# Attention block with two layer norms: the transpose of an iteration's row maxima placed behind the first turn of the next iteration

## What is computed

```python
x = x + attention(layernorm(x), Wq, Wk, Wv, Wo, bo)    # 16 heads of 16, causal softmax, scale 0.25
x = x + ffn(layernorm(x), rhs)

def ffn(lhs, rhs):        # rows of lhs and columns of rhs rounded to int8 by their largest magnitude
    acc = q_lhs @ q_rhs
    return acc * lhs_scale * rhs_scale
```

## Time and profile before

| | us |
|---|---|
| median of 3 runs | 1652.0 |
| lowest and highest | 1650.38, 1652.75 |
| the profiled execution, its own time | 1652.5 |
| its span, first to last instruction | 1650.7 |
| PE busy | 1562.4 (95%) |
| DVE busy | 1523.9 (92%) |
| ACT busy | 1363.3 (83%) |
| POOL busy | 275.4 (17%) |
| reductions of the max pass (line 356): 960 into `pmax`, 128 into `pblk` | 1101.0 and 151.8 |

### The profile page before, as it was taken

How to read it: one execution, slowest core, us unless ns; L and a number is a source line. 1 busy time by engine, 2 the same in 40 slices (tenths; PEclk the granted TensorE clock), 3 DMA queues, 4 the chain that set the end, 5 groups by cost and what they waited for, 6 DMA issues and landing times.

```text
span 1650.7 us, 40675 instructions
## 1 busy us (share of the span) xinstructions
PE 1562.4 (95%) x16715; PEld 623.3 (38%) x16715; DVE 1523.9 (92%) x1839; ACT 1363.3 (83%) x2659; POOL 275.4 (17%) x394
## 2 busy tenths in 40 slices
PE   5999999999999999999999999999999999999965
PEld 3555433333333333333333333333333333444433
DVE  5889989999999999999999999999999999488876
ACT  3656579999999999999999999999999999777641
POOL 3334201211112020202020202020202020100120
PEclk9999989999999999999999999999999999999986
DMA  3464301111211121212121212121212241035431
GB/s 112 149 195 141 107 23 35 35 35 34 61 47 61 47 69 47 64 45 67 47 61 48 73 37 77 34 77 36 77 29 79 46 139 34 32 107 160 146 106 62
DMA packets 105684, 118.84 MB, mean 72 GB/s; under 512 B 20696, under 2 KB 87580, under 8 KB 105500
## 3 DMA queue, kind: packets, MB, share of 16 engines
q1 hardware_dynamic: 105500, 116.25, 24.1%
HBM read 66.81 MB, written 48.76 MB: 70 GB/s over the span
## 4 chain that ended last, share of the span: by engine, by line
DVE 56%; PE 28%; ACT 1%; issue 1%; DMA 0%; SPq 0%; POOL 0%; DVEq 0%; ACTq 0%
DVE pmax L356 47%; PE psum L1155 12%; PE psum L1136 6%; DVE pblk L356 4%; PE psum L1196 3%; PE psum L264 3%; PE psum L278 2%; PE psum L283 2%; DVE V L1459 1%; DVE V L1440 1%; DVE V L1447 1%; DVE f_amax L1465 1%; ACT prob L1328 1%; PE psum L1220 1%; PE psum L1209 0%
## 5 line engine op out<-in xcount | busy, mean ns | idle before, releaser
L1328 ACT ACTIVATE prob<-psum 128x512 f32<-128x512 f32 (+1 forms) x2304 | 1180.8, 575 | 139.5 <-PE psum L1136 116.0
L356 DVE TENSOR_REDUCE pmax<-psum 128x2 f32<-128x1024 f32 (+1 forms) x960 | 1101.0, 1216 | 13.7 <-PE psum L283 7.0
L1155 PE MATMUL psum<-prob,V 128*32 128x256 f32 x8704 | 677.3, 391 | 0.0
L1136 PE MATMUL psum<-Q,K 50*128 50x512 f16 (+3 forms) x2560 | 465.9, 350 | 3.7 <-PEq L480 1.1
L1394 POOL TENSOR_SCALAR_AFFINE_SELECT prob<-prob 128x512 f32<-128x512 f32 x256 | 159.7, 636 | 1186.8 <-ACT prob L1328 1184.2
L264 PE MATMUL psum<-K,Q 48*128 48x512 f16 x1536 | 298.6, 385 | 12.6 <-DVE pmax L356 12.6
L1155 PEld LDWEIGHTS psum<-prob,V 128*32 128x32 f32 x8704 | 181.6, 108 | 294.9 <-issue 214.6
L1136 PEld LDWEIGHTS psum<-Q,K 50*128 50x128 f16 x2560 | 174.6, 94 | 251.5 <-ACT prob L1328 184.2
L264 PEld LDWEIGHTS psum<-K,Q 48*128 48x128 f16 x1536 | 74.3, 93 | 257.9 <-DVE pmax L356 209.7
L356 DVE TENSOR_REDUCE pblk<-psum 128x8 f32<-128x1024 f32 x128 | 151.8, 1219 | 5.9 <-PE psum L283 5.8
L283 PE MATMUL psum<-K,Q 48*128 48x512 f16 (+3 forms) x1024 | 128.5, 298 | 0.0
(11 more groups left out here) (122 smaller groups left out, 697.2 us busy)
## 6 DMA issues: line engine op xcount, KB each, us to landing
f_x<-in_L_attn_x SPq DMA_DIRECT2D x32, 512.0 KB, 5.2
unnormalised<-ust SPq DMA_DIRECT2D x64, 256.0 KB, 2.8
q_parts<-part SPq DMA_DIRECT2D x64, 128.0 KB
k_parts<-part SPq DMA_DIRECT2D x64, 128.0 KB
Q<-q_parts SPq DMA_DIRECT2D x128, 64.0 KB, 2.5
K<-k_parts SPq DMA_DIRECT2D x128, 64.0 KB, 2.1
out<-V SPq DMA_DIRECT2D x16, 512.0 KB, 3.3
f_rs<-inverse_sums SPq DMA_DIRECT2D x28, 256.0 KB
```

Source lines behind the costliest of these rows:

```text
L356: nc.vector.tensor_reduce(to, of, axis=AX.X, op=ALU.max).then_inc(M.mx_free, 1)
L1136: m = nc.tensor.matmul(PS[:, SB + i % RING, at:at + n], K[it % 2][rows, pair, kb * P:(kb + 1) * P], Q[it % 2][rows, pair, (c + 1) * CH - n ...
L1155: m = nc.tensor.matmul(PS[32 * h:32 * h + 32, UB, to:to + n], V[:, it // NG * NT + kb, col:col + 32], prob[(it * NSTEP + k) % PRING][:, h, ...
L1328: nc.scalar.activation(prob[g % PRING][:, h, 0:n], PS[:, SB + i % RING, 0:n], ACT.Exp, scale=by).then_inc(exp_done, 1)
```

## The change

The order of `TURNS` changes. The tail of iterations 1 to 14 moves from behind its own last turn to behind the first turn of the next iteration. The tails of iterations 0 and 15 stay. `TURNS` keeps its length, `BEFORE` its rows. DVE still combines the maxima directly behind the last turn of an iteration: at the first turn of the next one, ahead of its reduction (`combined_before` says at which turn which combination stands).

```diff
     for it in range(ITS):
-        turns += [(it, kind) for kind in (KINDS if it else sorted(KINDS, key=lambda kind: max(chunks_of(kind))))]
-        tail.append(len(turns))
-        turns.append((it, None))
+        for i, kind in enumerate(KINDS if it else sorted(KINDS, key=lambda kind: max(chunks_of(kind)))):
+            turns.append((it, kind))
+            if it >= 2 and i == 0:
+                tail.append(len(turns))
+                turns.append((it - 1, None))
+        if it in (0, ITS - 1):
+            tail.append(len(turns))
+            turns.append((it, None))
     return turns, tail
+
+
+def combined_before(n):
+
+    if TURNS[n][1] is None:
+        return TURNS[n][0] if TURNS[n][0] in (0, ITS - 1) else None
+    return TURNS[n + 1][0] if TURNS[n + 1][1] is None and TURNS[n + 1][0] < TURNS[n][0] else None
...
-assert sum(row[0] + row[2] for row in BEFORE) == TAIL[1] - TAIL[0] and sum(row[1] for row in BEFORE) == len(BLOCKS)
+assert sum(row[0] + row[2] for row in BEFORE) == TAIL[2] - TAIL[1] and sum(row[1] for row in BEFORE) == len(BLOCKS)
...
-    base = TAIL[0] + 1 + AHEAD + it * (TAIL[1] - TAIL[0])
+    base = TAIL[0] + 1 + AHEAD + it * (TAIL[2] - TAIL[1])
...
 def combine_maxima(nc, dve, it, M):
...
-    dve.wait_ge(M.mx_free, TAIL[it])
+    dve.wait_ge(M.mx_free, TAIL[it] - (0 if it in (0, ITS - 1) else 1))
...
 def max_turn_on_dve(nc, dve, n, PS, M):
...
     at = M.MB + 2 * (n % 2)
+    if combined_before(n) is not None:
+        combine_maxima(nc, dve, combined_before(n), M)
     if kind is None:
-        combine_maxima(nc, dve, it, M)
         take_maxima(nc, dve, it, PS, M)
         return
```

## The result

| | before | after |
|---|---|---|
| median, us | 1651.78 (4 runs, 1650.38 to 1652.75) | 1663.74 (4 runs, 1662.08 to 1666.31) |
| the profiled execution, its own time | 1652.5 | 1663.89 |
| its span | 1650.7 | 1661.9 |
| ratio of the medians | | 1.0072, 95% interval 1.0056 to 1.0088 |

The account below looks back on a forecast made before the run. The prediction took TensorE, not VectorE, to bound the kernel where the transpose stands. A net delay of 0.88 us at 14 places gave 12.3 us, added to 1652.0 for 1664; the 8 in 10 range was 1653 to 1669.

Parts of the forecast that it names:

- Steps 1 and 2: At each moved place: F0 takes T's place on TensorE, the next scores start 0.14 later, VectorE starts F0 0.39 earlier.
- F0: The first turn of the next iteration, whose place on TensorE is exchanged with T's; its reduction on VectorE takes 1.23.
- Step 3: T waits for nothing on TensorE; its copy follows F0's reduction, and the 0.72 idle time before the copy goes.
- T: The transpose on TensorE with its copy on VectorE, moved at 14 places (iterations 1 to 14).
- Steps 4 and 5: TensorE stands still about 1.1 us before F1; 0.23 comes back at S1; the turn after F1 is 0.88 later.
- F1: The second turn of the next iteration; after the change it waits on TensorE for F0's reduction.
- S1: The second score pair behind T on TensorE (849.95), held up by exponentials; expected to take 0.32 instead of 0.55.
- Step 6: Behind the place: VectorE's back-to-back reductions move as a block, so no slack takes in the 0.88.
- Step 7: SP issues the four transfers of the maxima 1.4 us later, covered by 4 us before scores read them.
- A: Rival: VectorE bounds the whole place, so starting F0 0.39 earlier saves 5.5 us, at most 15.0; chance 0.12.
- B: Rival: no change that shows, 1652, as later gaps take in the delay; chance 0.08.
- C: Rival: the stall costs TensorE its clock at the 14 places, 70 us, 1723; chance 0.02.

Follow-up runs that it names:

- the short F0 in the kernel before: The kernel before, with F0's reduction cut to one of its two banks in iterations 2 to 15: 1652.27 us, ratio to before 1.0007.
- the fitted order: The changed kernel with F0 issued one block of value products earlier on TensorE, and F1, the next turn and the blocks spread between scores: 1652.48 us, ratio 1.0009.

## Why the prediction was right

It was right by its own steps; here is each against the trace of after, with the 5.32 taken off. That the median came out within 0.3 us of the forecast is luck, since its four runs spread over 4 us; the period is the better measure.

Steps 1 and 2. S0 at 849.27 (expected 849.25), F0 on VectorE at 849.49 (849.48), its end at 850.72 (850.71).

Step 3. T at 849.59, 0.11 later than expected: I gave S0 0.23, its time ahead of a turn, but ahead of the transpose it takes 0.32 (854.59 to 854.91). It was hidden in the wait that followed. The copy starts at 850.63, slightly inside the recorded end of F0's reduction, and waits for nothing.

Steps 4 and 5. F1 at 850.77 (850.76), S1 at 851.09 (851.07), values 851.40 (851.39), S2 852.41 (852.40), F2 852.64 (852.63), its reduction 853.25 (853.24). A part of the stall comes back at S1, as said: ScalarE has caught up by then, and S1 takes 0.31 instead of 0.55.

Step 6. Nothing is won back: the period is 81.99, where 81.98 was said.

With weight loads pulled ahead of running matmuls (the Trainium skill, TensorE: Matmul & The Clock Gate, "Architectural detail: the array is 16× 32×32, not 1× 128×128") it would have been 10.6 us by the prediction's estimate. The trace shows nothing of it at this place: the loads that stand behind the semaphore wait start with the release, at 856.09, after 1.09 us of idle time.

Step 7. SP's timeline shows the four transfers of the maxima:

```profile
856.25 2.50 SPq L239 DMA_DIRECT2D Q<-mT  x4
```

They start at 850.93 on the clock of before, 1.33 later than there (1.4 expected), and no score matmul waits for them: in the tile view of `Q` over the whole execution, what ends the idle times before its instructions is never a transfer.

The sum. 14 x 0.89 = 12.5 us by the periods; 12.0 between the medians. The two profiles differ by 11.4. What is missing lies ahead of the 14 places. The first copy of `mT` comes at 282.0 instead of 281.6, 0.4 later, though its place alone makes it 1.35 later (850.63 for 849.28), so the changed kernel was some 0.95 us ahead when it got there. Over 205 to 230 us the mean granted clock is 0.80 before and 0.86 after: an estimate from these two is a stretch at half clock shorter by some 3 us (0.06 of 25 us, over 0.5), which is 1.5 us of time. Whether that is chance was not tested.

Not as said: ScalarE's idle time ended by score matmuls was to grow by nearly 1 us a place; the list of waits has 116.0 before and 124.5 after, 0.6 a place. ScalarE's wait before S1's exponentials is 0.73, and the one before S2's is 0.25 where it was 0.33: 0.65 net. In the first part of TensorE's stall it still has exponentials to do: its four of 853.81 last until 856.09.

The rivals. A (VectorE is the bound, faster) is refuted by the short F0 in the kernel before, and again by the fitted order, which gave VectorE its F0 early. B (taken in later) is refuted by the period. C (the clock) is refuted by the granted clock of 1.00. The Trainium skill (TensorE: Matmul & The Clock Gate, "A second HAM failure mode: psum-queue depth-cycling") speaks of frequent short idle times between matmul groups that make the clock go up and down; the 14 gaps of 0.95 us here, one in each 82, didn't.

## What to carry to other kernels

With two buffers, the wait of step n is on step n-2, so a short step in the sequence (here a transpose with a 0.2 us copy) is what gives its neighbours slack; move it, and a long step comes to stand where the short one was. Before an idle time of one engine is removed, look in the chain of waits for who bounds that stretch: 0.72 us of idle VectorE was free, and 0.95 us of idle TensorE cost 0.89. And where an order is written out by hand for several engines, an element moved in one of them has to be fitted in the others too, and even then the gain is bounded by the work of the one that is full.

## What the runs showed that was not expected

The same pair of score matmuls, S1, took 0.33 us on TensorE where a block of value products stood on both sides of it, 0.55 behind F0 and F1 in the kernel before, and 0.91 directly behind the transpose, 0.48 us after the pair before it: held by the exponentials for 0.6 us, though ScalarE as a whole is busy only 83% of the span. A move on one engine sets how another one's back-pressure is felt. And within one trace the 14 places repeat to 0.03 us in a period of 81, while the runs on the same chip spread over 8 us and more (1647.07 to 1655.18 for the kernel before in the last comparison). A period tells small changes apart that the time of the whole doesn't; a difference as small as the 0.02 between 81.10 and 81.08 would still need a second profile of each kernel.
